# An order of its own for the steps behind the last evacuation, in a pipelined two-layer block

## The chip, the cores and the metric

The kernel runs on one core of one Trainium2 chip. The metric is device microseconds of one execution, less is better. TensorE does matrix products, VectorE, ScalarE and GpSimd the elementwise work, and SyncE (SP) issues the DMAs. The four compute engines and SP each run an own list of instructions in its written order, and wait for each other on semaphores.

## The reference

x has 4096 tokens of 512 numbers. Cut to what matters:

```python
u   = x + x @ (W + delta_W).T                     # 512 x 512
x1  = (u - mean(u)) / sqrt(var(u) + 1e-5)
z   = x1 @ tern(W_syn).T + b_syn                  # 512 -> 2048, weights in {-s, 0, s}
thr = the 204th largest of a token's 2048 z       # k = int(2048 * 0.1)
h   = where(z >= thr, relu(z), 0)
v   = layernorm(x1 + h @ tern(W_out).T + b_out) * gamma + beta
out = layernorm(v)
```

The threshold is the hard part: for each token the value of rank 204 of 2048 has to be found.

## The kernel before

The tokens are cut into 32 tiles of 128 (`TILES`), one per partition row. All engines run the same software pipeline: one loop over s from -3 (`FIRST`) to 38 (`LAST`), and in step s every engine works at different tiles. Tile t is normalised in step t-2, multiplied to z (`mm2`) in t-1, evacuated to SBUF (`evac`, L629) in t, selected in t+4 (`L_SEL`), multiplied back (`mm3_hi`, `mm3_lo`) in t+5, normalised in t+6 and t+7 and stored in t+7. `live(t)` says whether t is a tile. From s = 32 (`TILES`) on there is no new z: steps 32 to 38 only finish tiles 25 to 31.

The threshold is found by counting. ScalarE counts (`count(t, r)`, L481, one pass over 2048 numbers) how many z lie above a guess; round r of tile t is in step t+r, r from 0 to 4, so that a step has up to five counts. After all counts of step s-1 GpSimd's `update(s)` (L365 to L384, eleven small instructions that depend on each other) moves the guesses of all five tiles in flight at once, and raises `updated`. In step s, with f = s-4, VectorE then takes the z below the guess (`below(f)`, L605, waits for `updated`), the eight largest of these (`top8`, L610), picks the wanted one by the last count (`select`, L617 to L622; L620 makes `ok`), and TensorE adds the `ok` of all rows with a matmul of one column (`flags`, L776). `general` (L642) reads that sum for a branch that covers the rare rows where the guess was too far off. Then `hidden` (L663) zeroes what is under the threshold.

h goes to TensorE in two halves of 16 bits: ScalarE's `hi_h` (L505) makes the upper, VectorE's `lo_h` (L599) the rest. SP transposes both by DMA (L257, L263), and `mm3_hi` and `mm3_lo` multiply them, 16 matmuls each, into one of three PSUM banks `o_ps`. VectorE's `add_r` (L682) adds the residual, with GpSimd's `add_bout` (L346) as its input. The norms: GpSimd's `means` (L329), ScalarE's `square2` and `square3` (L456, L464), GpSimd's `scales` (L336, L338, L341), then VectorE's `centre` and `add_v` (L668, L675) for the inner one and ScalarE's `ln3_out` (L498) for the outer one, whose result SP stores (L268).

The order inside a step is written out by hand for each engine. TensorE: `mm3_hi`, `mm3_lo` of tile s-5, `flags` of s-4, then `mm1` and `mm2`. VectorE: `lo_h(s-5)`, `evac(s)`, `below`, `top8`, `select` of s-4, `general`, `hidden`, `centre`, `add_v` of s-6, `add_r(s-5)`. ScalarE: the counts of rounds 4 and 3, `ln3_out(s-7)`, the counts of rounds 2 and 1, `hi_h(s-4)`, the count of round 0, and the squares of step s+1. GpSimd: `update(s)`, `reset`, `scales(s)`, `add_bout`, `add_beta`, `means(s+1)`. SP: `transpose_lo(s-5)`, loads, `transpose_x`, `store(s-7)`, `transpose_hi(s-4)`.

Of the kernel before, what the change touches and what calls it, by code (L numbers as in the profile page):

```python
# [13 lines left out]
TILES = TOK // P  # L14
# [17 lines left out]
ROUNDS = 5  # L32
# [11 lines left out]
L_SEL, L_MM3, L_LN2, L_OUT = 4, 5, 6, 7  # L44
A_LN1, A_MM1 = 2, 3
FIRST, LAST = -A_MM1, TILES - 1 + L_OUT
# [4 lines left out]
def live(t):  # L51
    return 0 <= t < TILES
# [7 lines left out]
def postln_kernel(nc, x, xT, wT, dwT, w_synT, b_syn, w_outT, b_out, gamma, beta, out):  # L60
    ctx = ExitStack()
    with ctx:
# [222 lines left out]
        def _(pool):  # L285
# [108 lines left out]
            for s in range(FIRST, LAST + 1):  # L394
                if s == 0:
                    sigma()
                if 1 <= s <= TILES + ROUNDS - 2:
                    update(s)
                if live(s):
                    reset(s)  # L400
                if live(s + A_LN1) or live(s - L_LN2) or live(s - L_OUT):
                    scales(s)
                l, d = s + 1 - L_MM3, s + 1 - L_LN2
                if live(s - L_SEL):
                    pool.wait_ge(h_made, s - L_SEL + 1)
                if live(l):
                    if l == 0:
                        pool.wait_ge(vecs_made, 1)
                    add_bout(l)
                if live(d):  # L410
                    add_beta(d)
                if live(d) or live(d - 1):
                    means(s + 1)

        @block.scalar
        def _(act):
# [84 lines left out]
            def hi_h(t):  # L501
# [2 lines left out]
                wait(act, hiT[t % 2], 16 * (t // 2))  # L504
                a_.activation(hh[:, t % 2, 0, :], z_sb[:, t % ZS, :], ACT.Copy).then_inc(h_hi, 1)  # L505

            for s in range(FIRST, LAST + 1):
                m, f, n = s, s - L_SEL, s + 1
                if live(f):
                    count(f, 4)  # L510
                if live(s - 3):
                    count(s - 3, 3)
                if live(s + A_LN1):
                    ln1_out(s, s + A_LN1)
                    hi_x(s + A_LN1)
                if live(s - L_OUT):
                    ln3_out(s, s - L_OUT)
                if live(s - 2):
                    count(s - 2, 2)
                if live(s - 1):  # L520
                    count(s - 1, 1)
                if live(f):
                    hi_h(f)
                if s == -1:
                    for k in range(KD):
                        sum_nnz(k)
                    for k in range(KD):
                        sum_out(k)
                if live(m):
                    count(m, 0)  # L530
                if live(n + A_LN1):
                    square1(n, n + A_LN1)
                if live(n - L_LN2):
                    square2(n, n - L_LN2)
                if live(n - L_OUT):
                    square3(n, n - L_OUT)

        @block.vector
        def _(dve):
# [153 lines left out]
                if k == KD - 2:  # L693
                    lo_x(0)

            for s in range(FIRST, LAST + 1):
                m, f, l, d = s, s - L_SEL, s - L_MM3, s - L_LN2
                if live(l):
                    lo_h(l)
                if s == 0:  # L700
                    scaling()
                if live(m):
                    evac(m, 0)
                    evac(m, 1)
                if s == 0:
                    spread()
                    out_part()
                if live(f):
                    below(f)
                    top8(f)  # L710
                    select(f)
                if live(s + A_LN1) and s + A_LN1 > 0:
                    lo_x(s + A_LN1)
                if s == 1:
                    out_scale()
                    out_weights(0)
                    out_weights(1)
                if s in (2, 3):
                    out_weights(s)
                if live(f):  # L720
                    general(f)
                    hidden(f)
                if live(d):
                    centre(s, d)
                    add_v(s, d)
                if live(l):
                    add_r(s, l)

        @block.tensor
        def _(pe):  # L730
# [54 lines left out]

            for s in range(FIRST, LAST + 1):
                f, l, n = s - L_SEL, s - L_MM3, s + 1
                if live(l):
                    if l == 0:
                        pe.wait_ge(t_out_made, KD)  # L790
                    mm3_hi(l)
                    mm3_lo(l)
                if live(f):
                    flags(s, f)
                if live(s + A_MM1):
                    mm1(s + A_MM1)
                if live(n):
                    if n == 0:
                        pe.wait_ge(t_syn_made, KD)
                    mm2(n, 0)  # L800
                    mm2(n, 1)
                if n == 0:
                    total(o_ps[1][:, 0:KD], nsyn[:, :], 2)
                if n == 1:
                    total(o_ps[2][:, 0:1], part[:, 1:2], 3)
# [28 lines left out]
```

## Time and profile before

| | |
|---|---|
| median of 3 runs | 716.71 us (715.83 to 717.73) |
| profiled execution | 715.85 us |
| its span, first to last instruction | 714.1 us |
| TensorE busy | 586.6 us (82%) |
| VectorE busy | 534.7 us (75%) |
| ScalarE busy | 538.3 us (75%) |
| GpSimd busy | 357.1 us (50%) |
| mean granted clock of TensorE | 0.939 of full speed |

The profile's page cuts the span into 40 equal slices of 17.9 us. In its rows each digit is a busy share in tenths; the row PEclk is the clock that TensorE was granted, in tenths of 2.4 GHz:

```profile
PE   0065888799999999999999999999999988444443
DVE  1726275588888888888888888888888898666651
ACT  5229547768899899999899998999989988864322
POOL 0820253234555565555555555555555555555541
PEclk9999899799999999999999999999999999777766
```

PE is TensorE, PEld its weight loads, DVE VectorE, ACT ScalarE, POOL GpSimd, SPq and DVEq the queues of SP and VectorE. The rows further down are of three kinds. A listing in order of time gives start and duration in us, engine, line of the kernel, operation, output<-inputs, shapes, and in brackets how long the engine was idle before and what ended that. The chain of waits gives start, duration and the work that the end of the kernel depended on.

### The profile page before, as it was taken

What the parts mean: (1) busy time and instruction counts of PE and PEld (TensorE: products, weight loads), DVE (VectorE), ACT (ScalarE), POOL (GpSimd) and SP (SyncE); (2) the same over time, 40 slices, a digit from 0 to 9 for tenths busy, and PEclk for the clock granted to TensorE, in tenths of its full rate; (3) what the DMA queues carried; (4) which work ended last, traced back from release to release, by engine and by line L of the source; (5) the groups of instructions that cost most, each with busy time, mean ns of one, the idle gap of its engine ahead of it and who ended that gap; (6) DMA issues with size and microseconds to landing.
All of it is one profiled execution on the core that took longest, in us unless ns stands there. A gap on an engine that the chain in (4) does not pass through costs nothing.

```text
span 714.1 us, 8153 instructions
## 1 busy us (share of the span) xinstructions
PE 586.6 (82%) x2374; PEld 255.9 (36%) x2374; DVE 534.7 (75%) x618; ACT 538.3 (75%) x677; POOL 357.1 (50%) x729
## 2 busy tenths in 40 slices
PE   0065888799999999999999999999999988444443
PEld 0022333344444444444444444444444433111111
DVE  1726275588888888888888888888888898666651
ACT  5229547768899899999899998999989988864322
POOL 0820253234555565555555555555555555555541
PEclk9999899799999999999999999999999999777766
DMA  9911111444646455554445554545444453333330
GB/s 346 380 41 41 48 31 42 88 74 76 124 92 121 91 120 92 115 99 109 102 106 113 94 118 90 119 88 118 90 89 90 89 90 84 80 73 59 74 88 30
DMA packets 184336, 71.61 MB, mean 100 GB/s; under 512 B 167904, under 2 KB 176096, under 8 KB 183648
## 3 DMA queue, kind: packets, MB, share of 16 engines
q1 hardware_dynamic: 184288, 71.06, 44.8%
q8 instruction: 19, 0.31, 0.2%
q14 instruction: 29, 0.24, 0.1%
HBM read 20.71 MB, written 8.39 MB: 41 GB/s over the span
## 4 chain that ended last, share of the span: by engine, by line
POOL 24%; issue 21%; PE 15%; DMA 5%; DVE 4%; ACT 2%; DVEq 1%; POOLq 0%; ACTq 0%
PE o_ps L762 6%; POOL nmean L329 6%; DMA hT<-hh 5%; PE o_ps L768 5%; POOL b L341 4%; POOL x1b L346 3%; PE z_ps L752 3%; POOL rs L338 3%; DVE z_sb L663 2%; ACT hh L505 2%; POOL x1g L350 2%; PE u_ps L738 2%; POOL dev L365 1%; POOL tmp L370 1%; POOL t_col L384 1%
## 5 line engine op out<-in xcount | busy, mean ns | idle before, releaser
L481 ACT ACTIVATE junk<-z_sb,t_col 128x2048 f16<-128x2048 f32 x128 | 254.8, 1992 | 43.1 <-POOL t_col L384 43.1
L752 PE MATMUL z_ps<-t_syn,xhT 128*128 128x512 f16 x1024 | 226.2, 379 | 0.6 <-issue 0.6
L762 PE MATMUL o_ps<-t_out,hT 128*128 128x512 f16 x512 | 126.5, 404 | 54.0 <-DMA hT<-hh 54.0
L738 PE MATMUL u_ps<-weff,xT_sb 128*128 128x512 f32 x256 | 129.0, 650 | 38.4 <-ACT weff L429 21.1
L346 POOL TENSOR_TENSOR x1b<-x1s,vecs 128x512 f32<-128x512 f32 x32 | 40.7, 1271 | 233.2 <-DVE z_sb L663 233.2
L752 PEld LDWEIGHTS z_ps<-t_syn,xhT 128*128 128x128 f16 x1024 | 100.0, 98 | 131.4 <-issue 18.1
L629 DVE SCALAR_TENSOR_TENSOR z_sb<-z_ps,sc,bias_z 128x1024 f32<-128x1024 f32 x64 | 81.6, 1278 | 56.1 <-PE z_ps L752 56.1
L768 PE MATMUL o_ps<-t_out,hT 128*128 128x512 f16 x512 | 115.8, 379 | 0.7 <-DMA hT<-hh 0.7
L663 DVE SCALAR_TENSOR_TENSOR z_sb<-z_sb,thr 128x2048 f32<-128x2048 f32 x32 | 75.3, 2352 | 28.2 <-DVE flag L642 25.8
L762 PEld LDWEIGHTS o_ps<-t_out,hT 128*128 128x128 f16 x512 | 52.0, 103 | 122.6 <-DMA hT<-hh 56.0
L599 DVE TENSOR_TENSOR hh<-z_sb,hh 128x2048 f16<-128x2048 f32 x32 | 85.3, 2665 | 3.2 <-ACT hh L505 3.2
L505 ACT ACTIVATE hh<-z_sb 128x2048 f16<-128x2048 f32 x32 | 61.2, 1911 | 35.2 <-DVE z_sb L663 33.2
L605 DVE SCALAR_TENSOR_TENSOR w_sb<-z_sb,t_col 128x2048 f32<-128x2048 f32 x32 | 75.1, 2346 | 11.9 <-POOL t_col L384 11.9
L738 PEld LDWEIGHTS u_ps<-weff,xT_sb 128*128 128x128 f32 x256 | 50.1, 206 | 94.1 <-issue 72.1
L329 POOL TENSOR_SCALAR nmean<-sums 128x2 f32<-128x2 f32 x33 | 71.3, 2160 | 9.7 <-DVE o_ps L682 8.2
L610 DVE MAX8 m<-w_sb 128x8 f32<-128x2048 f32 x32 | 73.4, 2295 | 1.1
L768 PEld LDWEIGHTS o_ps<-t_out,hT 128*128 128x128 f16 x512 | 49.8, 98 | 61.9 <-DMA hT<-hh 2.2
L481 ACT ACTIVATE junk<-z_sb,start 128x2048 f16<-128x2048 f32 x32 | 63.6, 1988 | 2.9 <-DVE z_sb L629 2.9
L456 ACT ACTIVATE junk_ln<-o_ps,nmean 128x512 f16<-128x512 f32 x32 | 22.0, 687 | 31.9 <-POOL nmean L329 31.9
L338 POOL TENSOR_TENSOR rs<-var,cst 128x3 f32<-128x3 f32 x41 | 40.1, 978 | 3.4
L636 DVE TENSOR_TENSOR xh<-x1s,xh 128x512 f16<-128x512 f32 x32 | 22.0, 687 | 25.3 <-ACT xh L493 25.2
L350 POOL TENSOR_TENSOR x1g<-x1s,vecs 128x512 f32<-128x512 f32 x32 | 40.7, 1270 | 0.0
(106 smaller groups left out, 531.7 us busy)
## 6 DMA issues: line engine op xcount, KB each, us to landing
xT_sb<-in_xT SPq DMA_DIRECT2D x16, 512.0 KB, 4.8
out_y<-y_sb SPq DMA_DIRECT2D x32, 256.0 KB, 2.4
z_sb<-in_w_synT SPq DMA_DIRECT2D x4, 1024.0 KB, 8.0
z_sb<-in_w_outT SPq DMA_DIRECT2D x2, 1024.0 KB, 14.7
hh<-in_w_outT SPq DMA_DIRECT2D x2, 1024.0 KB, 14.3
weff<-in_wT SPq DMA_DIRECT2D x1, 1024.0 KB, 13.4
w_sb<-in_dwT SPq DMA_DIRECT2D x1, 1024.0 KB, 15.6
bias_z<-in_b_syn SPq DMA_DIRECT2D x1, 1024.0 KB, 14.0
```

What stands on the lines that cost most here:

```text
L329: g.tensor_scalar(nmean[:, j, :], sums[:, j, :], -1.0 / D, None, ALU.mult).then_inc(neg_means, 1)
L481: a_.activation(junk[:, done[0] % 2, :], z_sb[:, t % ZS, :], ACT.Sign, bias=bias, scale=-1.0, accum_out=signs[:, t % CS:t % CS + 1]).then_ ...
L505: a_.activation(hh[:, t % 2, 0, :], z_sb[:, t % ZS, :], ACT.Copy).then_inc(h_hi, 1)
L599: v.tensor_tensor(hh[:, j, 1, :], z_sb[:, t % ZS, :], hh[:, j, 0, :], ALU.subtract).then_inc(h_lo, 1)
L605: v.scalar_tensor_tensor(w_sb[:, :], z, t_col[:, t % CS:t % CS + 1], z, ALU.is_le, ALU.mult)\
L610: v.max(out=m8[:, t % 2, :], in_=w_sb[:, :]).then_inc(max8_done, 1)
L629: v.scalar_tensor_tensor(z_sb[:, t % ZS, c * HALF:(c + 1) * HALF], z_ps[:, c, :], sc[:, 7:8], bias_z[:, c * HALF:(c + 1) * HALF], ALU.mult ...
L663: v.scalar_tensor_tensor(z, z, thr[:, t % 2:t % 2 + 1], z, ALU.is_ge, ALU.mult).then_inc(h_made, 1)
L738: last = mm(u_ps[:, :], xT_sb[:, j, k, (t % 2) * P:(t % 2 + 1) * P], weff[:, k, :], start=k == 0, stop=k == KD - 1)
L752: last = mm(z_ps[:, c, b * BANK:(b + 1) * BANK], xhT[:, j, h * KD + k, :], t_syn[:, k, n0:n0 + BANK], start=k == 0 and h == 0, stop=k == K ...
L762: mm(o_ps[t % OS][:, :], hT[:, j, 0, c, :], t_out[:, c, :], start=c == 0, stop=False)
L768: last = mm(o_ps[t % OS][:, :], hT[:, j, 1, c, :], t_out[:, c, :], start=False, stop=c == KN - 1)
```

## The change

Nothing is added or removed; in the steps from 32 on instructions change places in the lists of four engines.

- GpSimd: `update(32)` moves from the start of step 32 to step 31, between `scales(31)` and the wait for `h_made`; `update(33)` to `update(35)` move from the start of their step to the start of the one before.
- ScalarE: from step 32 on the squares of step s stand in step s, behind the counts, instead of at the end of step s-1; `ln3_out` comes behind them, before `hi_h`.
- VectorE: from step 32 on `below` comes first, then `lo_h`, `top8` and the rest.
- TensorE: from step 32 on `flags` comes before `mm3_hi` and `mm3_lo`.

```diff
@@ -394,12 +394,16 @@
             for s in range(FIRST, LAST + 1):
                 if s == 0:
                     sigma()
-                if 1 <= s <= TILES + ROUNDS - 2:
+                if 1 <= s < TILES:
                     update(s)
                 if live(s):
                     reset(s)
+                if TILES < s + 1 <= TILES + ROUNDS - 2:
+                    update(s + 1)
                 if live(s + A_LN1) or live(s - L_LN2) or live(s - L_OUT):
                     scales(s)
+                if s + 1 == TILES:
+                    update(s + 1)
                 l, d = s + 1 - L_MM3, s + 1 - L_LN2
                 if live(s - L_SEL):
                     pool.wait_ge(h_made, s - L_SEL + 1)
@@ -504,6 +508,14 @@
                 wait(act, hiT[t % 2], 16 * (t // 2))
                 a_.activation(hh[:, t % 2, 0, :], z_sb[:, t % ZS, :], ACT.Copy).then_inc(h_hi, 1)
 
+            def squares(s):
+                if live(s + A_LN1):
+                    square1(s, s + A_LN1)
+                if live(s - L_LN2):
+                    square2(s, s - L_LN2)
+                if live(s - L_OUT):
+                    square3(s, s - L_OUT)
+
             for s in range(FIRST, LAST + 1):
                 m, f, n = s, s - L_SEL, s + 1
                 if live(f):
@@ -513,12 +525,16 @@
                 if live(s + A_LN1):
                     ln1_out(s, s + A_LN1)
                     hi_x(s + A_LN1)
-                if live(s - L_OUT):
+                if live(s - L_OUT) and s < TILES:
                     ln3_out(s, s - L_OUT)
                 if live(s - 2):
                     count(s - 2, 2)
                 if live(s - 1):
                     count(s - 1, 1)
+                if s >= TILES:
+                    squares(s)
+                    if live(s - L_OUT):
+                        ln3_out(s, s - L_OUT)
                 if live(f):
                     hi_h(f)
                 if s == -1:
@@ -528,12 +544,8 @@
                         sum_out(k)
                 if live(m):
                     count(m, 0)
-                if live(n + A_LN1):
-                    square1(n, n + A_LN1)
-                if live(n - L_LN2):
-                    square2(n, n - L_LN2)
-                if live(n - L_OUT):
-                    square3(n, n - L_OUT)
+                if n < TILES:
+                    squares(n)
 
         @block.vector
         def _(dve):
@@ -693,7 +705,7 @@
                 if k == KD - 2:
                     lo_x(0)
 
-            for s in range(FIRST, LAST + 1):
+            for s in range(FIRST, TILES):
                 m, f, l, d = s, s - L_SEL, s - L_MM3, s - L_LN2
                 if live(l):
                     lo_h(l)
@@ -726,6 +738,23 @@
                 if live(l):
                     add_r(s, l)
 
+            for s in range(TILES, LAST + 1):
+                f, l, d = s - L_SEL, s - L_MM3, s - L_LN2
+                if live(f):
+                    below(f)
+                if live(l):
+                    lo_h(l)
+                if live(f):
+                    top8(f)
+                    select(f)
+                    general(f)
+                    hidden(f)
+                if live(d):
+                    centre(s, d)
+                    add_v(s, d)
+                if live(l):
+                    add_r(s, l)
+
         @block.tensor
         def _(pe):
             mm = nc.tensor.matmul
@@ -785,12 +814,14 @@
 
             for s in range(FIRST, LAST + 1):
                 f, l, n = s - L_SEL, s - L_MM3, s + 1
+                if live(f) and s >= TILES:
+                    flags(s, f)
                 if live(l):
                     if l == 0:
                         pe.wait_ge(t_out_made, KD)
                     mm3_hi(l)
                     mm3_lo(l)
-                if live(f):
+                if live(f) and s < TILES:
                     flags(s, f)
                 if live(s + A_MM1):
                     mm1(s + A_MM1)
```

## Rows read from the trace of the kernel before

**Rows 1.** VectorE's instructions in order of time (start, us, line), steps 32 to 36.

```profile
617.73 2.35 DVE L605 SCALAR_TENSOR_TENSOR w_sb<-z_sb,t_col 128x2048 f32<-128x2048 f32 x1 [2.79 <-POOL t_col L384]
...
622.71 0.22 DVE L620 SCALAR_TENSOR_TENSOR ok<-m,t_col,hit 128x1 f32<-128x1 f32 x1
...
630.11 0.75 DVE L682 SCALAR_TENSOR_TENSOR o_ps<-o_ps,sc,x1b 128x512 f32<-128x512 f32 x1
...
630.78 2.66 DVE L599 TENSOR_TENSOR hh<-z_sb,hh 128x2048 f16<-128x2048 f32 x1
...
636.21 2.38 DVE L605 SCALAR_TENSOR_TENSOR w_sb<-z_sb,t_col 128x2048 f32<-128x2048 f32 x1 [2.78 <-POOL t_col L384]
...
644.79 0.15 DVE L642 CAST flag<-z_ps 1x1 int32<-1x1 f32 x1 [3.20 <-PE z_ps L776]
...
674.31 2.35 DVE L605 SCALAR_TENSOR_TENSOR w_sb<-z_sb,t_col 128x2048 f32<-128x2048 f32 x1 [2.78 <-POOL t_col L384]
...
688.04 2.66 DVE L599 TENSOR_TENSOR hh<-z_sb,hh 128x2048 f16<-128x2048 f32 x1
...
702.36 0.76 DVE L682 SCALAR_TENSOR_TENSOR o_ps<-o_ps,sc,x1b 128x512 f32<-128x512 f32 x1 [7.09 <-PE o_ps L768]
```

**Rows 2.** The chain of work that ended last: start, us, what; step 33.

```profile
645.80 2.36 DVE z_sb L663
...
650.12 4.28 DMA hT<-hh
```

**Rows 3.** TensorE's matmuls in order of time, all from 599 us on that bear.

```profile
599.63 3.63 PE L762 MATMUL o_ps<-t_out,hT 128*128 128x512 f16 x16 [2.32 <-DMA hT<-hh]
...
616.58 5.18 PE L762 MATMUL o_ps<-t_out,hT 128*128 128x512 f16 x16 [9.75 <-DMA hT<-hh]
...
634.98 6.20 PE L762 MATMUL o_ps<-t_out,hT 128*128 128x512 f16 x16 [9.65 <-DMA hT<-hh]
...
654.45 5.02 PE L762 MATMUL o_ps<-t_out,hT 128*128 128x512 f16 x16 [9.70 <-DMA hT<-hh]
...
673.09 5.92 PE L762 MATMUL o_ps<-t_out,hT 128*128 128x512 f16 x16 [10.05 <-DMA hT<-hh]
...
692.33 6.54 PE L762 MATMUL o_ps<-t_out,hT 128*128 128x512 f16 x16 [9.75 <-DMA hT<-hh]
...
698.71 3.62 PE L768 MATMUL o_ps<-t_out,hT 128*128 128x512 f16 x16
```

**Rows 4.** ScalarE's instructions in order of time, end of step 31.

```profile
613.96 0.19 ACT L481 ACTIVATION_READ_ACCUMULATOR junk<-z_sb,start 128x1 f32 x1
```

**Rows 5.** GpSimd's instructions in order of time, steps 32 and 36.

```profile
615.12 0.24 POOL L365 TENSOR_SCALAR dev<-signs 128x5 f32<-128x5 f32 x1
...
617.78 2.36 POOL L336 TENSOR_SCALAR var<-ss 128x3 f32<-128x3 f32 x1
...
703.27 0.24 POOL L329 TENSOR_SCALAR nmean<-sums 128x2 f32<-128x2 f32 x1 [8.16 <-DVE o_ps L682]
```

**Rows 6.** All engines in order of time, 128 to 137 us.

```profile
128.67 0.22 DVE L620 SCALAR_TENSOR_TENSOR ok<-m,t_col,hit 128x1 f32<-128x1 f32 x1
...
128.95 0.19 PE L776 MATMUL z_ps<-ok,ones 128*1 128x1 f32 x2 [6.49 <-DVE ok L620]
...
129.07 6.66 PE L738 MATMUL u_ps<-weff,xT_sb 128*128 128x512 f32 x8
...
135.18 2.29 DVE L599 TENSOR_TENSOR hh<-z_sb,hh 128x2048 f16<-128x2048 f32 x1 [1.98 <-ACT hh L505]
```

**Rows 7.** GpSimd in order of time, during the set-up.

```profile
19.14 9.98 POOL L304 TENSOR_TENSOR weff<-weff,w_sb 128x512 f32<-128x512 f32 x4 [16.95 <-DMA w_sb<-in_dwT]
```

**Rows 8.** VectorE in order of time, during the set-up.

```profile
22.57 3.23 DVE L551 SCALAR_TENSOR_TENSOR t_syn<-z_sb,sc,hT 128x2048 f16<-128x2048 f32 x1
```

**Rows 9.** TensorE in order of time, 85 to 105 us.

```profile
85.85 3.68 PE L738 MATMUL u_ps<-weff,xT_sb 128*128 128x512 f32 x8
...
99.85 5.37 PE L738 MATMUL u_ps<-weff,xT_sb 128*128 128x512 f32 x8 [3.41 <-ACT x1s L488]
```

## The prediction, made before the changed kernel ran

> **What bounds the kernel now.** The page first: the 40 slices show every engine near nine tenths in the middle and all of them thin in the last seven, with TensorE's granted clock down to six or seven tenths there. The change touches only that end, so the rest of the reading is the instructions in order of time from 598 us on. A step is named by the number s of the loop that all engines share; 32 is the first one without an evacuation of z. VectorE's rows give the pace: `below` (L605) of steps 32, 33 and 35 starts at 617.73, 636.21 and 674.31 [rows 1], so steps 32 to 34 take 18.9 us each on average. The chain of waits says why. TensorE runs the 32 matmuls of tile s-5 and only then the one of the flag, and VectorE's L642 stood still 3.2 us for it [rows 1]; behind the flag come `hidden` (2.36), `hi_h` on ScalarE, 4.28 us of the transposing DMA, and then the next 32 matmuls [rows 2]. So this is one closed loop: matmuls, flag, hidden, transpose, matmuls. In each of its turns the first part of the matmuls is slow: 16 of them take 5.18, 6.20, 5.02, 5.92 and 6.54 us, against 3.63 for the burst of step 31 that followed 2.32 us of idleness [rows 3]. The first matmuls of these five run at the 1.2 GHz level, after a wait of 9.65 to 10.05 us, and the second sixteen at 2.4 GHz (3.62 us [rows 3]).
>
> **The change, part by part.** No instruction is added or taken away; every one listed keeps its duration. I work out when `below` starts in each step (T32, T33, ...), then the last tile.
>
> *Update at once.* `update(32)` is eleven tiny GpSimd instructions. They may start when ScalarE's last count of step 31 is in: its accumulator read ends at 614.15 [rows 4]. Before, they sat behind `add_bout`, `add_beta` and `means`, and started at 615.12 [rows 5]. From their start to that of `below` are 2.61 us (615.12 to 617.73 [rows 5, 1]). With 0.1 us for the hand-over (an estimate; the new gap can't be below zero, and 0.97, that of now, bounds it above), T32 = 614.15 + 0.1 + 2.61 = 616.9 instead of 617.73. In step 31 the three instructions of GpSimd now queue behind the update; the first user of them is a square of ScalarE at about 625, so they have eight microseconds. In steps 32 to 34 `update(s+1)` starts after the counts and the selection, overlaps `hidden`, and `scales` with the reciprocal roots stands behind it on GpSimd. VectorE's `centre` waits for that: flag and update start at T+7.5 (below); `hidden` runs from T+8.7 (0.2 to the cast, 1.0 from cast to `hidden`, 644.79 to 645.80 [rows 1, 2]) to T+11.1 and holds the update up; the 1.4 us that are left of it end at T+12.5, the roots some 1.5 later (as in the last steps of the listing), then `centre` and `add_v` 1.5: VectorE is free for `add_r` at about T+15.5.
>
> *Flag first.* The flag's matmul no longer waits for 32 others. But TensorE works in order, so the 32 matmuls of tile s-5 now wait for the flag, that is for `select`, and so for T; their operands have been there since long. And `add_r(s-5)`, the last instruction of the step on VectorE, waits for them, with the next step's `below` queued behind it. This closes a new loop, which I think sets the pace: matmuls, `add_r`, `below`, `lo_h`, `top8`, `select`, flag, matmuls. SP loses nothing by it: `transpose_lo`, the store and `transpose_hi` keep their order, and the store of the moved `ln3_out` (after the roots, about T+15) comes ahead of `transpose_hi(s-4)`, whose 16 matmuls can't start before the next flag, at T+25.
>
> *Below first.* `lo_h` moves from the idle time ahead of `below`, where it cost nothing (VectorE then waited 2.8 us), to between `below` and `top8`, where it costs its length. It takes 2.66 where a GpSimd addition overlaps its start [rows 1], and 2.29 alone [rows 6]; its follower starts 0.07 sooner, so 2.22. From the start of `below` to L620, which makes `ok`, are 4.98 us now (617.73 to 622.71 [rows 1]); with `lo_h` 7.20.
>
> *The new loop.* L620 to flag 0.28 (128.67 to 128.95), flag to the next matmul 0.12 [rows 6]. The first sixteen: the mean of the five rows is 5.77, less the overlap of 0.16 with the second sixteen (692.33 + 6.54 against 698.71 [rows 3]): 5.61. From the start of the second sixteen to `add_r` 3.65 (698.71 to 702.36 [rows 3, 1]). From `add_r` to what follows it 0.67 (630.11 to 630.78 [rows 1]). Sum: 7.20 + 0.28 + 0.12 + 5.61 + 3.65 + 0.67 = 17.53, against 18.9. The matmuls are there at T+16.86, 1.4 us after the T+15.5 of the path through `centre`, which is next in line.
>
> *Norms last.* The two squares stand before `ln3_out` and `hi_h` on ScalarE, after the counts. The delay of `hi_h` (it starts at about T+15.4 instead of T+11.1, and takes 1.96 with the hand-over, 648.16 to 650.12 [rows 2]) is covered: with 4.28 of DMA its transpose is there at T+21.6, and the next flag comes at T+25. Cost nothing; without that cover the whole delay would count.
>
> *One collision.* The GpSimd work that the update has put back in step 32 (`add_bout` first) waits while `below` runs: one instruction of GpSimd that started with `below` took 2.36 instead of some 0.2 [rows 5]. When `below` ends, `lo_h` comes at once and wants the same. In the set-up four additions of GpSimd of this size took 9.98 together [rows 7], and the two-input instruction of VectorE between them 3.23 [rows 8] instead of 2.35 as `below` of equal width [rows 1]: they take turns. So `lo_h` of step 32 pays 0.88. The Trainium skill ("SBUF — State Buffer", "Who interferes with whom") says that whichever starts first holds the shared ports for its whole instruction; by that the whole of the addition could fall on `lo_h`, more than 0.88. The rows show 0.88, and I take these.
>
> T33 = 616.9 + 17.53 + 0.88 = 635.3 (now 636.21), T34 = 652.8, T35 = 670.4 (now 674.31: 3.9 gained).
>
> *The last tile.* `add_r(30)` starts at 670.4 + 16.86 = 687.2 and `lo_h(31)`, behind it, at 687.9. Now it starts at 688.04 [rows 1], because there it doesn't wait for the matmuls: nearly all the lead is given back at this place. Alone it takes 2.29: 690.2; the transpose lands 4.3 later (as [rows 2]), and the second sixteen of tile 31 start at 694.6. The first sixteen, whose transpose is there at 670.4 + 11.1 + 1.96 + 4.3 = 687.8, run right behind tile 30 at full rate until 691. So TensorE is idle some 3.8 us before the last sixteen. At full rate these take 3.65 (end 698.2), and if they are as slow as the slowest sixteen, 6.54 (end 701.1). The nearest row: 3.41 us of idleness made a burst of eight 5.37 long, against 3.68 [rows 9], 1.7 more. I take this: 699.9. The skill ("TensorE: Matmul & The Clock Gate", "HAM oscillation — how this bites in real kernels") says that a stream that stops for its operands comes back at the lower clock; by it the last sixteen begin slow, and the trace bears that out for the waits of 3.41 and of ten, not for 2.32. `add_r(31)` then starts at 699.95 instead of 702.36 [rows 1], and all behind it is unchanged: 2.4 us gained.
>
> The profiled execution took 715.85 us for a span of 714.1; by the sum the changed one takes 713.4. It lies 0.86 below the median of the three runs, 716.71, which I take as the base: 714.3.
>
> **The rivals.**
>
> *A, both ends kind (gain 4 to 5).* The last sixteen run at full rate (1.7 more gained), or the first sixteen are short as in 654.45 (5.02), 0.75 less per step, until the path through `centre` stops it at T+15.5. For it: 2.32 us of idleness cost nothing [rows 3]. Against it: 3.41 did [rows 9]. Time 716.7 - 4.5 = 712.2.
>
> *B, the ports take it (no change).* `means` of GpSimd starts 0.91 us after `add_r` (702.36 to 703.27 [rows 1, 5]), that is 0.24 after `below` starts, and so waits for the ports in every step. If it makes `lo_h` pay 0.88 each time, as the additions did, steps 33 to 35 lose 3 x 0.88 = 2.6 and the gain is gone: 716.9. For it: the taking of turns [rows 8]. Against: this one is five times shorter than those additions when free (0.24 [rows 5]). A last burst at the slow end (1.2 less) together with long first sixteens ends at the same place.
>
> *C, slower.* The matmuls were in the loop before too, but now they have VectorE's `lo_h` in it with them, and what they lose is lost four times and once more at the end. Its point: if TensorE's clock stays at 1.2 GHz through the second sixteen too (6.54 instead of 3.62), the four bursts cost 11.7 more: 714.3 + 11.7 = 726. It is slower than now from 0.6 us per burst on, 9.86 instead of 9.26 from first matmul to `add_r`. Against it: in all five bursts the second sixteen were at full rate; one of the five, the last, lasted 10.03 in this sense.
>
> **How the numbers follow.** The sum 0.5, A 0.2, B 0.22, C 0.08. The sum's own range: 0.6 us up or down for the mean of the first sixteen, over four bursts some 1.3, and 1.2 to 4.1 of gain from the last: 712.5 to 716. With A and B, and the hand-over bound, 711 to 717.2. A measurement of this kernel tells 0.3%, that is 2.15 us, from no change. Within the sum's case a little over half lies beyond it (0.29), all of A does (0.2): faster 0.49. The rest of the sum and B give 0.43 for no change, C 0.08.
>
> **What would show it.** `below(28)` near 616.9 with VectorE idle in front of it; each flag's matmul 0.3 us after L620, and the 32 others right behind; `add_r` of steps 32 to 35 waiting for TensorE, 16.9 us after `below`; steps of 17.5 us; `lo_h(31)` at about 688 again; idleness of 3.8 us before the last sixteen matmuls. Wrong it would be if `add_r` waits for `centre` or `add_v` instead, if `lo_h` is 3.2 us long in every step, or if the steps are not shorter than 18.9.

## The result

Nine runs of each: the changed kernel takes 712.25 us in the median (712.04 to 715.02), the kernel before 715.83 (713.65 to 717.99). The ratio is 0.9959, interval 0.9940 to 0.9978: 2.9 us faster by the ratio, 3.6 by the medians. When it ran again in a later group, beside another set of the kernel before, it was 0.9934 (0.9911 to 0.9957). Forecast were 2.4 us less than before and a time of 714.3, in a range from 711.0 to 717.2; the forecast started from 716.71, the median of three runs of the kernel before, which with nine is 715.83. The profiled execution has a span of 710.4 us, against 714.1.

The page of the changed kernel, the 40 slices: TensorE is still thin in the last six, with its clock between six and eight tenths.

```profile
PE   0066888799999999999999999999999988245572
...
DVE  0726275678888888888888888888888897677751
...
PEclk9999899799999999999999999999999999778786
```

VectorE of the changed kernel in order of time; the lines have moved by 12: L617 is `below`, L611 `lo_h`, L632 makes `ok`, L694 is `add_r`. These answer to [rows 1].

```profile
612.58 0.76 DVE L694 SCALAR_TENSOR_TENSOR o_ps<-o_ps,sc,x1b 128x512 f32<-128x512 f32 x1
...
617.82 2.35 DVE L617 SCALAR_TENSOR_TENSOR w_sb<-z_sb,t_col 128x2048 f32<-128x2048 f32 x1 [4.43 <-POOL t_col L384]
620.09 3.35 DVE L611 TENSOR_TENSOR hh<-z_sb,hh 128x2048 f16<-128x2048 f32 x1
...
625.95 0.22 DVE L632 SCALAR_TENSOR_TENSOR ok<-m,t_col,hit 128x1 f32<-128x1 f32 x1
...
635.07 0.76 DVE L694 SCALAR_TENSOR_TENSOR o_ps<-o_ps,sc,x1b 128x512 f32<-128x512 f32 x1 [1.28 <-PE o_ps L797]
...
635.75 2.35 DVE L617 SCALAR_TENSOR_TENSOR w_sb<-z_sb,t_col 128x2048 f32<-128x2048 f32 x1
...
669.72 2.35 DVE L617 SCALAR_TENSOR_TENSOR w_sb<-z_sb,t_col 128x2048 f32<-128x2048 f32 x1
...
686.76 2.29 DVE L611 TENSOR_TENSOR hh<-z_sb,hh 128x2048 f16<-128x2048 f32 x1
...
698.73 0.76 DVE L694 SCALAR_TENSOR_TENSOR o_ps<-o_ps,sc,x1b 128x512 f32<-128x512 f32 x1 [5.14 <-PE o_ps L797]
```

The wait of `add_r` is ended by TensorE (L797) in every step, `below` follows it after 0.68 us without idleness, and the steps are 17.93, 16.96 and 17.01 us long, instead of 18.9. `lo_h` of step 32 takes 3.35.

TensorE of the changed kernel, answering to [rows 3]; L805 is the flag's matmul, L791 and L797 are the two sixteens:

```profile
626.22 0.19 PE L805 MATMUL z_ps<-ok,ones 128*1 128x1 f32 x2 [18.42 <-DVE ok L632]
626.35 5.24 PE L791 MATMUL o_ps<-t_out,hT 128*128 128x512 f16 x16
631.42 3.62 PE L797 MATMUL o_ps<-t_out,hT 128*128 128x512 f16 x16
...
643.20 5.34 PE L791 MATMUL o_ps<-t_out,hT 128*128 128x512 f16 x16
...
677.17 5.42 PE L791 MATMUL o_ps<-t_out,hT 128*128 128x512 f16 x16
...
687.23 3.63 PE L791 MATMUL o_ps<-t_out,hT 128*128 128x512 f16 x16 [1.18 <-DMA hT<-hh]
693.38 5.31 PE L797 MATMUL o_ps<-t_out,hT 128*128 128x512 f16 x16 [2.52 <-DMA hT<-hh]
```

The flag comes 0.27 after L632 (625.95 to 626.22), the 32 matmuls 0.13 later. The first sixteen of steps 32 to 35 take 5.2 to 5.4, and the last burst of all takes 5.31 for sixteen that otherwise take 3.62. GpSimd, answering to [rows 5]:

```profile
615.21 0.25 POOL L365 TENSOR_SCALAR dev<-signs 128x5 f32<-128x5 f32 x1 [9.43 <-ACT junk L485]
...
617.87 3.42 POOL L346 TENSOR_TENSOR x1b<-x1s,vecs 128x512 f32<-128x512 f32 x1
...
635.98 2.22 POOL L329 TENSOR_SCALAR nmean<-sums 128x2 f32<-128x2 f32 x1 [1.11 <-DVE o_ps L694]
```

The update starts at 615.21, 2.63 behind `add_r(26)` instead of 3.52. `add_bout` (L346), started with `below`, is held for 3.42 us.

The executions differ ahead of the change as well: `add_r(26)`, the last instruction of step 31 on VectorE, starts at 611.60 in the trace of before and at 612.58 in that of after, and between 609.6 and 615.5 in the others here, whose first 600 us are the same program. These differences are as large as most effects below. So I compare traces by the time from the start of `add_r(26)` to the end of the span, called the tail: 102.5 us before, 97.8 after (and 97.7 in the second trace). The change is worth 4.7 us by the traces, and 2.9 to 4.7 by the two ratios.

### The profile page after: what moved, and what is told of

Same layout as the page of the kernel before. It is cut to its first block, busy times and chain, and to the rows that moved or that the text cites. A ratio compares the mean times of both kernels' runs of the same rounds, so it can differ in the third digit from the quotient of the medians.

```text
span 710.4 us, 8153 instructions
## 1 busy us (share of the span) xinstructions
PE 585.6 (82%) x2374; PEld 255.7 (36%) x2374; DVE 534.0 (75%) x618; ACT 537.5 (76%) x677; POOL 357.1 (50%) x729
## 4 chain that ended last, share of the span: by engine, by line
PE 27%; POOL 18%; issue 17%; DVE 6%; DMA 3%; ACT 1%; DVEq 0%; POOLq 0%; ACTq 0%
PE z_ps L781 8%; PE o_ps L791 8%; PE o_ps L797 8%; POOL nmean L329 4%; PE u_ps L767 4%; DMA hT<-hh 3%; POOL b L341 3%; POOL x1b L346 2%; POOL rs L338 2%; DVE m L622 2%; POOL x1g L350 1%; DVE w_sb L617 1%; DVE z_sb L675 1%; DVE hh L611 1%; ACT hh L509 1%
## 5 line engine op out<-in xcount | busy, mean ns | idle before, releaser
L346 POOL TENSOR_TENSOR x1b<-x1s,vecs 128x512 f32<-128x512 f32 x32 | 42.8, 1339 | 202.8 <-DVE z_sb L675 202.7
L791 PE MATMUL o_ps<-t_out,hT 128*128 128x512 f16 x512 | 124.1, 399 | 6.3 <-DMA hT<-hh 6.3
L641 DVE SCALAR_TENSOR_TENSOR z_sb<-z_ps,sc,bias_z 128x1024 f32<-128x1024 f32 x64 | 81.6, 1278 | 56.0 <-PE z_ps L781 56.0
L797 PE MATMUL o_ps<-t_out,hT 128*128 128x512 f16 x512 | 117.4, 383 | 3.2 <-DMA hT<-hh 3.2
L611 DVE TENSOR_TENSOR hh<-z_sb,hh 128x2048 f16<-128x2048 f32 x32 | 84.5, 2639 | 3.2 <-ACT hh L509 3.2
L617 DVE SCALAR_TENSOR_TENSOR w_sb<-z_sb,t_col 128x2048 f32<-128x2048 f32 x32 | 75.0, 2344 | 5.2 <-POOL t_col L384 5.2
L791 PEld LDWEIGHTS o_ps<-t_out,hT 128*128 128x128 f16 x512 | 51.5, 102 | 73.3 <-issue 11.1
L329 POOL TENSOR_SCALAR nmean<-sums 128x2 f32<-128x2 f32 x33 | 69.0, 2090 | 14.8 <-DVE o_ps L694 13.2
L797 PEld LDWEIGHTS o_ps<-t_out,hT 128*128 128x128 f16 x512 | 50.3, 99 | 65.7 <-DMA hT<-hh 4.7
L805 PE MATMUL z_ps<-ok,ones 128*1 128x1 f32 x64 | 6.0, 164 | 49.0 <-DVE ok L632 49.0
L502 ACT ACTIVATE y_sb<-o_ps,b,rs 128x512 f32<-128x512 f32 x32 | 24.5, 765 | 28.2 <-POOL b L341 28.2
L350 POOL TENSOR_TENSOR x1g<-x1s,vecs 128x512 f32<-128x512 f32 x32 | 42.7, 1335 | 0.0
## 6 DMA issues: line engine op xcount, KB each, us to landing
z_sb<-in_w_outT SPq DMA_DIRECT2D x2, 1024.0 KB, 14.9
w_sb<-in_dwT SPq DMA_DIRECT2D x1, 1024.0 KB, 15.5
```

The costliest lines, as they stand in the source:

```text
L329: g.tensor_scalar(nmean[:, j, :], sums[:, j, :], -1.0 / D, None, ALU.mult).then_inc(neg_means, 1)
L611: v.tensor_tensor(hh[:, j, 1, :], z_sb[:, t % ZS, :], hh[:, j, 0, :], ALU.subtract).then_inc(h_lo, 1)
L617: v.scalar_tensor_tensor(w_sb[:, :], z, t_col[:, t % CS:t % CS + 1], z, ALU.is_le, ALU.mult)\
L641: v.scalar_tensor_tensor(z_sb[:, t % ZS, c * HALF:(c + 1) * HALF], z_ps[:, c, :], sc[:, 7:8], bias_z[:, c * HALF:(c + 1) * HALF], ALU.mult ...
L791: mm(o_ps[t % OS][:, :], hT[:, j, 0, c, :], t_out[:, c, :], start=c == 0, stop=False)
L797: last = mm(o_ps[t % OS][:, :], hT[:, j, 1, c, :], t_out[:, c, :], start=False, stop=c == KN - 1)
```

## The experiments

All ratios are to the kernel before, run on the same chip in the same group. The groups are: after; e1 to e4_no_below; e5, e6 and v2; after_again, e4_again, e7 and v3. The tail and the steps are those of one profiled execution of each.

| kernel | ratio, interval | tail, us | `below` to `below`, steps 32, 33, 34 |
|---|---|---|---|
| before | 1 | 102.5 | 18.48, 19.44, 18.66 |
| after | 0.9959, 0.9940 to 0.9978 | 97.8 | 17.93, 16.96, 17.01 |
| after_again | 0.9934, 0.9911 to 0.9957 | 97.7 | 17.87, 16.93, 16.99 |
| e1_flag_only | 1.0033, 0.9999 to 1.0066 | 104.0 | 19.94, 20.22, 20.35 |
| e2_batch_norms | 1.0042, 1.0022 to 1.0062 | 105.6 | 18.94, 19.76, 20.23 |
| e3_no_flag | 1.0089, 1.0061 to 1.0116 | 109.4 | 21.71, 18.42, 19.70 |
| e4_no_below | 0.9925, 0.9896 to 0.9953 | 97.8 | 17.58, 18.22, 17.66 |
| e4_again | 0.9889, 0.9860 to 0.9919 | 95.5 | 17.59, 16.93, 17.00 |
| e5_update_behind_beta | 0.9955, 0.9934 to 0.9975 | 98.6 | 17.84, 17.44, 17.26 |
| e6_warm | 0.9909, 0.9877 to 0.9941 | 96.4 | 18.46, 16.93, 16.93 |
| e7_warm34 | 0.9904, 0.9874 to 0.9934 | 95.1 | 18.02, 15.46, 15.88 |
| v2_shift | 0.9769, 0.9736 to 0.9802 | 85.8 | 11.27, 15.43, 14.73 |
| v3_means | 0.9705, 0.9674 to 0.9736 | 81.6 | 11.27, 13.51, 13.13 |

### One part at a time

**Flag first alone.** In the kernel before:

```diff
+                if live(f) and s >= TILES:
+                    flags(s, f)
                 if live(l):
 ...
-                if live(f):
+                if live(f) and s < TILES:
                     flags(s, f)
```

> Of the changed kernel only the order on TensorE: from step 32 on the flag's matmul stands in front of the 32 matmuls of tile s-5; update, squares and lo_h stay where they were. My theory (the matmuls now wait for the selection, and everything queued behind add_r on VectorE waits for the matmuls): add_r comes at T+14.7 instead of T+12.4, where T is the start of below; lo_h, means and the update follow it as before, 6.1 us up to the next below, so a step takes 20.8 us instead of 18.9. Three steps lose 5.9, the last tile gets 0.4 back: 5 us slower than before, about 721. Rival (each part of the change brings a share, and the flag, which waited 2 to 3 us for the matmuls in each step, is the largest): 2 to 4 us faster, about 713.

Measured: 1.0033, 2.4 us slower, with an interval that just touches 1. Its twelve runs fall into two groups, five from 714.46 to 714.95 and seven from 719.63 to 722.85, against a median of 715.97 for the kernel before beside them; the trace is of the second group (719.75), and its steps are 20.2 long on average. VectorE in its trace, step 32 (L682 is `add_r`, L599 `lo_h`, L605 `below`):

```profile
634.33 0.76 DVE L682 SCALAR_TENSOR_TENSOR o_ps<-o_ps,sc,x1b 128x512 f32<-128x512 f32 x1 [3.56 <-PE o_ps L768]
...
635.00 2.29 DVE L599 TENSOR_TENSOR hh<-z_sb,hh 128x2048 f16<-128x2048 f32 x1
640.07 2.35 DVE L605 SCALAR_TENSOR_TENSOR w_sb<-z_sb,t_col 128x2048 f32<-128x2048 f32 x1 [2.79 <-POOL t_col L384]
```

`add_r` waits 3.56 us for the matmuls, and the next `below` comes 5.74 later, with the update between them. The mechanism is there; I had its price too high. The bursts were 0.2 shorter than the mean I took, `below` came 0.4 sooner behind `add_r`, and the last tile gave 2.4 back instead of 0.4, both its sixteens taking 3.63. The rival, 2 to 4 us faster and about 713, falls: no run of the twelve was under 714.4. That the flag's place alone costs time is likely, and the interval does not quite show it.

**Update and norms alone**, TensorE and VectorE as before:

> Only the GpSimd and ScalarE parts of the change: update at once, and the squares and ln3_out behind the counts (the update at once can't stand without the latter, each would wait for the other). VectorE and TensorE keep their old order. My theory: the update is early, but lo_h, still in front of below, now waits for hi_h, which stands behind ln3_out and so behind the roots; below of the next step comes 19.2 us after the last, limited by flag, hidden, hi_h, transpose and matmuls as before. Slightly slower than before, by 1 to 2 us: 717 to 718. Rival (update at once alone takes the 2.8 us in front of below away in each step): 3 x 2.8 = 8 us faster, 708.

Measured: 1.0042, 3.0 us slower. Again the direction of my theory, and the reverse of the rival's 8 us gain; the steps are 19.6 long on average. The wait of `lo_h` for `hi_h` that I expected is there in step 33 only, 0.59 us. More came from the later `hi_h`: in step 33 TensorE waits 11.45 us for the transpose, where it waited 9.65 in the kernel before. The five first sixteens are 1.2 longer in sum in this trace, which is chance as far as I know.

**The change without flag first.**

> The changed kernel without its TensorE part: the flag waits for the 32 matmuls again. My theory: the loop is the old one (matmuls, flag, hidden, hi_h, transpose: 19.2 us), now with hi_h of step 32 later by the roots in front of it. The matmuls of tile 31 start some 4 us later than before (696 instead of 692 in the trace), the end is 3 us later: 719. Rival (the flag's place matters little, the gain comes from below first): as the changed kernel, 712.

Measured: 1.0089, 6.4 us slower, twice what I expected. The trace is of the slowest of its six runs (726.55). TensorE in its trace, step 32:

```profile
620.38 6.19 PE L791 MATMUL o_ps<-t_out,hT 128*128 128x512 f16 x16 [9.71 <-DMA hT<-hh]
630.66 6.17 PE L797 MATMUL o_ps<-t_out,hT 128*128 128x512 f16 x16 [4.09 <-DMA hT<-hh]
636.76 0.19 PE L805 MATMUL z_ps<-ok,ones 128*1 128x1 f32 x2
```

The second sixteen of tile 27 wait 4.09 us for their transpose, because `lo_h` now stands behind `below`, and after that wait they take 6.17 instead of 3.62. The flag stands behind them. I had left this out.

**The change without below first**, that is with `lo_h` in front:

```diff
-                if live(f):
-                    below(f)
                 if live(l):
                     lo_h(l)
                 if live(f):
+                    below(f)
                     top8(f)
```

> The changed kernel with lo_h in front of below again, as before. My theory: in a closed loop on VectorE the order of lo_h and below makes no difference to the length of a step (17.0), but in step 32 lo_h falls back into the 4.4 us of idleness in front of below, there it costs nothing and meets no addition of GpSimd, and the loop holds one lo_h less up to that of tile 31: 2.3 for it and 0.9 to 1.1 for the collision. 3.2 us faster than the changed kernel: 709, 6.5 below the kernel before. Rival (below first is what frees the selection and brings the gain): slower than the changed kernel by the 2.3 of each lo_h, 4 x 2.3 = 9, about 721.

Measured: 0.9925, 711.61 us, where I expected 709. The trace had no shorter tail than after. In it `lo_h` of step 33 waited for `hi_h`:

```profile
633.96 2.29 DVE L611 TENSOR_TENSOR hh<-z_sb,hh 128x2048 f16<-128x2048 f32 x1 [0.59 <-ACT hh L509]
```

and the first sixteens of steps 32 to 35 took 5.05, 6.48, 5.91 and 5.62, 23.1 in sum, where after has 21.4. It ran once more beside the changed kernel:

> lo_h in front of below again, as in e4_no_below, now beside the changed kernel. The first run gave 0.9925 against 0.9959 of another group. Its trace had the first sixteen matmuls of the four bursts 23.1 us long in sum (21.4 in the changed kernel) and lo_h of step 33 waiting 0.6 us for hi_h, which took most of the 3.2 us that I expected. My theory with these terms: 3.2 less 0.8 for the waits of the update and of lo_h, the bursts being drawn anew: 2 to 3 us faster than the changed kernel. Rival (lo_h's place makes no difference): the same time as the changed kernel.

> The changed kernel once more, so that it runs on the same chip as the three others of this group. Every theory: 0.996 of the kernel before, as measured.

Measured on one chip: 0.9889 against 0.9934 for the changed kernel, 3.2 us; the intervals (0.9860 to 0.9919, 0.9911 to 0.9957) overlap by a little. Its trace has a tail of 95.5 against 97.7, with equal steps in 33 and 34 (16.93 and 17.00 against 16.93 and 16.99): in a closed loop the order of `lo_h` and `below` makes no difference. The 2.2 us are those of one `lo_h`: with `lo_h(27)` in the idle time of step 32 there is one less of them on the way to `lo_h(31)`. Of the collision's 1.06 us little is left in the total: step 32 is 0.28 shorter, `below(28)` starts 0.19 later behind `add_r(26)`, and `lo_h(28)` waits 0.26 for `hi_h`. So update and norms lose alone, the flag's place alone gains nothing and likely loses, and the two gain together. That below first costs beside them is likely by the two ratios and the one trace of 95.5; the intervals overlap, and the trace of the first run shows no gain. Below first alone, and flag and below first without update and norms, weren't tried.

### The collision in step 32

```diff
-                if s + 1 == TILES:
-                    update(s + 1)
 ...
                 if live(d):
                     add_beta(d)
+                if s + 1 == TILES:
+                    update(s + 1)
```

> The changed kernel, with update(32) on GpSimd moved behind add_bout(27) and add_beta(26) of step 31 instead of in front of them; means(32) stays behind it. Those two additions then run before the counts of step 31 are in (from 611.3 to 613.8 in the changed kernel's time, the update starts at 615.2 anyway), and don't meet below and lo_h of step 32. My theory (the two engines take turns at the SBUF ports): lo_h(27) falls from 3.35 to 2.3 us, nothing else changes, 1.05 us faster than the changed kernel, 711.2. Rival (the meeting is only shown in the durations, another wait ends the step anyway): no change in the step of 17.9 us, 712.2.

Measured: 0.9955, no different from the changed kernel's 0.9959 and 0.9934; 1.05 us of gain were expected. Yet `lo_h` fell to 2.28 and the way from `below` to the flag from 8.40 to 7.36, as the theory has it. In this trace it is hidden by the first sixteens, which were 6.19, 5.83, 5.64 and 5.55 long, 1.8 more in sum than in after. By the total the test is inconclusive; the collision's price is shown by the row only.

### The clock of TensorE

Before each flag from step 32 on:

```diff
+                    if s == TILES:
+                        pe.wait_ge(z_evac, 2 * TILES)
+                        warm(28)
+                    warm(28)
                     flags(s, f)
```

`warm(n)` issues n matmuls of 512 columns into the unused second half of `z_ps`; `warm(10)` stands between the sixteens of tile 31.

> The changed kernel with 28 more matmuls of 512 columns in front of each flag from step 32 on (56 in step 32) and 10 between the two sixteens of tile 31, with results that nobody reads, in TensorE's idle time. My theory: the first sixteen of each step are on the path and slow (5.1 to 5.3 us to the second sixteen, instead of 3.45) only because TensorE's clock fell to 1.2 GHz in the 8 us of idleness before. Held busy it stays at 2.4 GHz: 1.7 us less per step, of which the path through centre (add_v ends 14.8 to 15.8 us after below in the changed trace) lets 1.4, 1.5, 1.5 and 1.8 through, and 1.7 in the last sixteen: 7.9 us faster than the changed kernel, 704.4. Rival (the slow stretch belongs to the start of a burst on these operands, or something else is already as late as the matmuls): no change, 712.2, or slower if the added matmuls delay the flag.

Measured: 0.9909, 708.92 us, where 704.4 was expected: the first sixteen of steps 33 to 35 still took 5.31. Only the last sixteen of tile 31 came at full rate (3.63 instead of 5.31), 1.7 us, of which 0.5 went in step 32, whose first sixteen took 5.77; the tail is 1.4 shorter than after's.

```profile
642.11 0.19 PE L805 MATMUL z_ps<-ok,ones 128*1 128x1 f32 x2 [2.00 <-DVE ok L632]
642.23 5.31 PE L791 MATMUL o_ps<-t_out,hT 128*128 128x512 f16 x16
```

Stretches of e6_warm with the granted clock (PEclk, a share of 2.4 GHz) and the number of TensorE's instructions in each:

```profile
core 0: us, PE busy (x) PEld busy (x) DVE busy (x) ACT busy (x) POOL busy (x), PEclk, DMA share, GB/s
634.00:640.10 6.10, 6.10 (x29) 2.52 (x27) 6.00 (x5) 6.10 (x9) 2.22 (x1) 1.00 0.46 86
642.20:643.40 1.20, 1.20 (x7) 0.55 (x6) 0.15 (x1) 0.00 (x0) 1.03 (x6) 0.78 0.85 161
643.40:646.80 3.40, 3.40 (x11) 1.23 (x10) 2.37 (x1) 0.00 (x0) 3.15 (x7) 0.58 0.00 0
```

The added matmuls ran at full rate (28 in 6.21 us, clock 1.00). After 2.00 us of idleness the real burst began at the full clock, and the clock fell inside its first 1.2 us (mean 0.78; 1.00 in the first half of them and 0.56 in the second). Then 34 instead of 28:

> As e6_warm with 34 added matmuls per step instead of 28 (68 in step 32). In e6_warm the added ones ran at full rate, 2.0 us of idleness were left ahead of each flag, and the first sixteen still took 5.31, the granted clock falling one microsecond into them. My theory (the clock falls because TensorE idles, even for 2 us at that place; it is not the flag nor the operands): with 0.7 us left the first sixteen take 3.6, steps of 15.1 to 15.5 us, 6 us in four steps, and with the last sixteen at full rate as in e6_warm 7 to 8 us faster than the changed kernel, 704.5. Rival (the slow stretch comes with the flag and the burst behind it): 5.3 again, as e6_warm, 709.

```profile
627.23 0.19 PE L805 MATMUL z_ps<-ok,ones 128*1 128x1 f32 x2 [3.64 <-DVE ok L632]
627.35 5.31 PE L791 MATMUL o_ps<-t_out,hT 128*128 128x512 f16 x16
...
644.17 0.19 PE L805 MATMUL z_ps<-ok,ones 128*1 128x1 f32 x2 [0.71 <-DVE ok L632]
644.29 3.63 PE L791 MATMUL o_ps<-t_out,hT 128*128 128x512 f16 x16
...
686.04 5.31 PE L791 MATMUL o_ps<-t_out,hT 128*128 128x512 f16 x16 [2.99 <-DMA hT<-hh]
691.19 2.32 PE L817 MATMUL z_ps<-t_syn,xhT 128*128 128x512 f16 x10
```

Measured: 0.9904, 708.9 us, some 2 us faster than the changed kernel beside it (0.9934), with overlapping intervals. In step 33, with 0.71 us of idleness in front, the first sixteen take 3.63 (1.27 and 1.34 us in steps 34 and 35, with the same result), and steps 33 and 34 fall to 15.46 and 15.88: the slow stretch belongs to TensorE's idleness, not to the flag or the operands. The expected 7 to 8 us did not come for three reasons that the trace shows: the burst of step 32 was slow still (3.64 us of idleness); in steps 33 and 34 `add_r` no longer waits for TensorE but follows `add_v` at once, 14.8 and 15.2 us after `below`; and at the end the first sixteen of tile 31 were slow after 2.99 us, with my ten added matmuls behind them on the path.

### Taking add_r out of the way

VectorE of v2_shift from step 32 on, cut to what matters; `norm(s)` is `centre`, `add_v`, `add_r` of step s. In the same run `lo_h(27)` stands in front of `below(28)`, and `ln3_out` and its store come one step later:

```diff
                 if live(f):
                     top8(f)
                     select(f)
+                if s > TILES:
+                    norm(s - 1)
+                if live(f):
                     general(f)
                     hidden(f)
-                if live(d):
-                    centre(s, d)
-                    add_v(s, d)
-                if live(l):
-                    add_r(s, l)
```

> The changed kernel, with centre, add_v and add_r of step s behind the selection of step s+1 on VectorE (from step 32 on), lo_h of step 32 in front of below, ln3_out of step s behind the counts of step s+1 on ScalarE, and SP's store one step later. My theory (what sets the step is add_r waiting for the matmuls with below behind it): below no longer waits for TensorE. A step is then limited by select, add_r, means, update and hidden: update(s+1) starts at about T+9.8, meets hidden at the ports and ends at T+14.6. Steps of 14.6 instead of 17.0 us, 7 us in three steps, 3.3 from lo_h in step 32, and 2.8 at the last tile, whose lo_h no longer stands behind add_r(30): 13 us faster than the changed kernel, 699 (698 to 703). Rival (the path through update and scales is the real bound, the matmuls only a microsecond later): 1 to 2 us per step at most, 706 to 708.

Measured: 0.9769, 698.63 us, as expected (699), with steps of 11.27, 15.43 and 14.73. GpSimd and VectorE in its trace, step 33 (L332 `means`, L368 to L387 the update, L679 `hidden`, L621 `below`):

```profile
637.47 0.26 POOL L332 TENSOR_SCALAR nmean<-sums 128x2 f32<-128x2 f32 x1 [2.45 <-DVE o_ps L698]
637.80 0.24 POOL L368 TENSOR_SCALAR dev<-signs 128x5 f32<-128x5 f32 x1
...
638.44 2.30 POOL L373 TENSOR_SCALAR tmp<-tmp 128x5 f32<-128x5 f32 x1
```

```profile
638.26 2.36 DVE L679 SCALAR_TENSOR_TENSOR z_sb<-z_sb,thr 128x2048 f32<-128x2048 f32 x1 [0.88 <-DVE flag L658]
642.45 2.38 DVE L621 SCALAR_TENSOR_TENSOR w_sb<-z_sb,t_col 128x2048 f32<-128x2048 f32 x1 [1.83 <-POOL t_col L387]
```

The update starts just ahead of `hidden`, is held for 2.3 us by it, and `below` waits 1.83 for it. So the update is the bound, and it went in front of `means`; the old call of `means(s + 1)` at the end of the step stays for the steps up to 31 only:

```diff
                 if TILES < s + 1 <= TILES + ROUNDS - 2:
                     update(s + 1)
+                if s > TILES:
+                    means(s)
```

> v2_shift, with means(s) on GpSimd behind update(s+1) instead of in front of it, for s over 32. In the trace of v2_shift means waits for add_r, the update behind it starts 0.6 us ahead of hidden and is then held up by it for 2.1 us; below of the next step waits 1.5 to 1.8 us for the update. My theory (the update is the bound now): it starts right behind select, beside centre, add_v and add_r, which don't hold GpSimd up, and is done before hidden starts. Steps of 12.9 to 13.3 us instead of 14.7 to 15.4, 5 us faster than v2_shift, about 694. Rival (the squares, which now get their means later, or the counts behind hi_h take its place): no faster than v2_shift, 698.6, and the wait in front of below is then for something else.

```profile
640.38 2.35 DVE L681 SCALAR_TENSOR_TENSOR z_sb<-z_sb,thr 128x2048 f32<-128x2048 f32 x1 [0.88 <-DVE flag L660]
642.65 2.34 DVE L623 SCALAR_TENSOR_TENSOR w_sb<-z_sb,t_col 128x2048 f32<-128x2048 f32 x1
```

Measured: 0.9705 (0.9674 to 0.9736), 695.07 us (694 expected), the fastest, 2.3% below the changed kernel run beside it. `below` (L623) follows `hidden` (L681) without a wait; the steps are 13.51 and 13.13. Neither the squares nor the counts took the update's place.

## Why the prediction was right

The new loop is the mechanism of the forecast, and it is what the trace shows. The size is not: by the tails the gain is nearly twice the 2.4 us of the sum. Taken from `add_r(26)`, so that the executions compare (it starts at 611.60 before, at 612.58 after):

- **Update at once.** `below(28)` 5.24 us after `add_r(26)` instead of 6.13: 0.89 gained, 0.83 forecast.
- **The new loop.** Forecast 17.53, measured 16.96 and 17.01. The hand-overs are as worked out (`below` to L632 in step 33 7.05, forecast 7.20); the term that was off is the first sixteen, 5.19 in the mean up to the second (626.35 to 631.42 the first of four), instead of 5.61. I had taken the mean of five rows that spread from 5.02 to 6.54, and no row told which of them would come.
- **The path through `centre` next in line.** `add_v` with its accumulator ended 14.9 to 16.0 us after `below` in steps 32 to 34, forecast 15.5, and e7_warm34 showed it to be the next bound.
- **The collision.** `lo_h(27)` 3.35 instead of 2.29: 1.06, forecast 0.88. The wait of `means` at `below` (635.98, 2.22 long) costs `lo_h` nothing, as the sum had it: rival B falls, whose condition was a `lo_h` of 3.2 us in every step.
- **The last tile.** `lo_h(31)` started 1.28 before that of the kernel before by the trace (686.76 against 688.04), 2.3 relative to `add_r(26)`; forecast was that nearly all is given back here (0.1). The difference is the shorter bursts (1.7) and the shorter way from `below` to L632 (0.15 in three steps). The idleness before the last sixteen was 2.52, not 3.8. The sum had let the first sixteen of tile 31 run until 691 right behind tile 30, against its own time for their transpose, 687.8, which leaves some 3.3; and as the loop was faster than forecast and the transpose was not, they waited 1.18 for it. The price was 5.31 - 3.62 = 1.7 as taken. Two stretches of it, PEclk again:

```profile
core 0: us, PE busy (x) PEld busy (x) DVE busy (x) ACT busy (x) POOL busy (x), PEclk, DMA share, GB/s
693.40:694.50 1.10, 1.10 (x6) 0.51 (x7) 0.19 (x2) 0.00 (x0) 0.02 (x1) 0.99 0.57 214
694.50:697.90 3.40, 3.40 (x10) 1.20 (x9) 0.00 (x0) 0.00 (x0) 0.00 (x0) 0.50 0.02 8
```

The clock was full (0.99) for the first 1.1 us and then at the 1.2 GHz level (0.50) for most of the burst.

By the traces `add_r(31)` comes 4.6 us sooner, where 2.4 were forecast: the right mechanism, with the term of the first sixteens too large by 0.42 in each of four bursts (1.7 in all). The ratios give 2.9 and 4.7. The time itself, 712.25, is that of rival A (712.2), and 0.9 us of its distance to 714.3 is the base, not the gain. Of A's two conditions neither held whole: the last sixteen ran at full rate in no trace of the changed kernel, and the first sixteen were shorter than in the sum by 0.42 where A had 0.75. That the first measurement lay as near to the forecast gain as 2.9 us is in part luck. Rival C (slower) needed the second sixteens at 1.2 GHz; that happened in e3_no_flag after 4.09 us of waiting, and in the changed kernel only for the last tile.

What I didn't see before: that below first, for which I had worked out a price of 2.22 per step, costs in step 32 only, and that leaving it out would be better. The sum held it already (in the new loop `lo_h` is on the path in every step, in either order, but ahead of step 32 VectorE still stands idle); I did not ask what its old place was worth.

## What to carry to other kernels

When an in-order engine ends its step with an instruction that waits for another engine, everything of the next step is behind that wait; look whether that instruction can go behind the next step's first work. In the changed kernel it was `add_r`, and moving it brought some 9 to 10 us: 12 (tails) to 13.6 (medians) between the changed kernel and v2_shift, less 2.2 to 3.2 for `lo_h`'s place. That is two to three times what all the moves of the change did. `ln3_out` and its store moved with it, and their share was not measured apart. In the kernel before `add_r` did not wait for TensorE in steps 32 to 35; what the same move brings there was not tried. Moves must be judged by the loop that they close: update with norms lost 3 us alone, flag first gained nothing alone, and together they gained.

## What the hardware showed

- The granted clock of TensorE fell after 2.00 us of idleness (e6_warm, three bursts of three) and after 2.52 us (after), and it fell inside the following burst, about a microsecond behind its start. The first sixteen of tile 31 were slow after 2.99 us too (e7_warm34). After 2.32 us in the main loop [rows 3], after 3.10 at the end of e1_flag_only, 3.15 at the end of v3_means and 3.34 at the end of v2_shift the burst ran at full rate:

```profile
677.28 3.63 PE L803 MATMUL o_ps<-t_out,hT 128*128 128x512 f16 x16 [3.34 <-DMA hT<-hh]
```

  What decides between them stays open; the length of the wait alone does not. In steps 32 to 35 of all the traces the first sixteen took from 5.02 to 6.55 us whenever TensorE had waited 2.00 us or more ahead of them. The nine runs of the changed kernel fall into two groups, six from 712.04 to 712.69 and three from 714.55 to 715.02; that these are two draws of those durations is likely, and not shown. For e1_flag_only the record has more: its five shorter runs have a mean granted clock of 0.947 and its seven longer ones 0.931 to 0.940.
- VectorE and GpSimd take turns instruction by instruction: a waiting GpSimd addition ran between two two-input instructions of VectorE and made the second 1.06 us longer, most of the 1.26 us that the addition takes alone. The Trainium skill ("SBUF — State Buffer", "Who interferes with whom") says that the loser is blocked for the whole instruction; the blocked `add_bout` of 3.42 us agrees, with its own 1.26 in it.
